# Gathers between two expert layers: from tile-by-tile waits to two in flight on two semaphores

## The chip, the core and the metric

The kernel runs on one core of a Trainium2 chip. The metric is the device time of one execution in microseconds (us); the time before is the median of three executions.

## The reference, cut to what matters

2048 tokens of 128 channels go through four residual layers: an attention, a mixture of 64 experts with 6 chosen per token, a table lookup, and a mixture of 8 experts with 2 chosen per token.

```python
x = x + attention(layernorm(x))
x = x + moe64(layernorm(x))      # sum over a token's 6 experts of weight * expert(token), + a shared expert
x = x + lookup(layernorm(x))     # offsets and weights from x, entries taken from x[0], summed, @ W_out + b_out
x = x + moe8(layernorm(x))       # sum over a token's 2 experts of weight * expert(token)
```

The change lies between the two expert layers: where each token's 6 expert outputs are brought together, and where the lookup and the router of the second mixture run on them.

## The kernel before

Tokens lie in 16 tiles of 128, in 4 chunks (q = 0 to 3) of 4 tiles. The engines have a program each, written out by hand, and wait for each other through named semaphores. An indirect DMA of the GpSimd engine (POOL) moves 128 rows, one per partition, by a column of row numbers, and adds 16 to a semaphore when it has landed.

1. During the attention, POOL scatters normalized tokens to slots in DRAM (`chunk_scatter`, line 1317, 96 scatters). Those of the chunks 0 to 2 wait on `exp_done`, three at a time; the last ones wait for nothing between them.
2. The 64 experts' layer runs over 80 pairs of slot blocks and writes its outputs to `y0_dram`.
3. Between the layers, `gathers(q, first, last)` (line 1374) brings the six outputs of each token into `GB`: 6 gathers for each tile, 24 for each chunk, 96 in all, 64 KB each. VectorE (DVE) waits for a tile's six in `combined(q, i)`, multiplies by the weights (line 1774), sums (1775), adds to `X` (1776) and takes statistics (1777). `moments_of` (1782) closes a chunk, POOL computes `rstd` from it (`chunk_scale`, 1382 and 1384), DVE normalizes (`scaled`, 1789), TensorE (PE) turns the rows (829), ScalarE (ACT) copies them out (1169), PE computes the lookup's offsets (839), DVE turns them into indices (`lookup_index`, 1799 to 1824), PE turns these (883), ACT casts them (1187), PE and DVE fill the lookup (`filled`, 905 and 1838 on), and `looked_up` adds the result. One chunk later the same tiles go through the second router (`router1_...`, lines 1870 to 1904; 1904 writes the slots).
4. `chunk_dispatch` (line 1392, 32 scatters) sends the tokens to the slots of the second mixture, whose 39 tiles end the kernel; each adds its rows to DRAM with one scatter (line 1418), which waits for the landing of the one two back, on `summed0` and `summed1` by turns.

What POOL does in the stretch between the layers is one queue in this order: 30 gathers (chunk 0 and the first tile of chunk 1), `chunk_scale` for chunk 0, 24 gathers, two `chunk_scale`, 24 gathers, two `chunk_scale`, 18 gathers, 4 dispatch scatters, two `chunk_scale`, the other scatters. DVE does, for q = 0 to 2: `scaled`, `combined(q + 1, 0)`, `lookup_index(q)`, `combined(q + 1, 1)`, `filled(q)`, `combined(q + 1, 2)`, `looked_up(q)`, `combined(q + 1, 3)`, with the router of the chunk before between them.

Of the kernel before, what the change touches and what calls it, by code (L numbers as in the profile page):

```python
# [12 lines left out]
P = 128  # L13
T = 2048
# [112 lines left out]
def build(nc, a, out):  # L127
# [12 lines left out]
    with ctx:  # L140
# [177 lines left out]

        TERMS_AT = (1, 2, 4, 5)
        SHIFT_AT = {1: 3, 3: 6}  # L320

        TURN_OF_LOOKUP = (0, 2, 4, 5)
# [167 lines left out]
        def _(pe):  # L490
# [67 lines left out]
            pe.wait_ge(sem("hxy_ready"), 1)  # L558
# [4 lines left out]
            last.then_inc(sem("corners_psum"), 1)  # L563
# [3 lines left out]
            pe.wait_ge(sem("corners_ready"), 1)  # L567
# [18 lines left out]
            pe.wait_ge(sem("mr_ready"), 1)  # L586
# [104 lines left out]
            pe.wait_ge(sem("q_final"), 1)  # L691
# [67 lines left out]
            mm(totals, cb("onesb"), earlier[:, :], start=False, stop=True, skip_group_check=True).then_inc(sem("totals0"), 1)  # L759
# [4 lines left out]
            pe.wait_ge(sem("table_cols"), 1)  # L764
# [87 lines left out]
            def counts1(q):  # L852
# [13 lines left out]
                if q == NC - 1:  # L866
                    for t in range(NT):
                        last = mm(totals1, cb("onesb"), MB[:, t, :], start=(t == 0), stop=(t == NT - 1), skip_group_check=True)
                    last.then_inc(sem("totals1"), 1)

            def tables():

                pe.wait_ge(sem("dx_ready"), 1)
                mm(PS[:, 7 * BANK:7 * BANK + P], cf("ones"), wout[:, :], start=True, stop=True)
                mm(PS[:, 7 * BANK + P:7 * BANK + P + 8], cf("selx"), dx[:, :], start=True, stop=True).then_inc(sem("tables_psum"), 1)
# [12 lines left out]
            def fills(q):  # L888
# [3 lines left out]
                for kind, i in FILLS:  # L892
# [16 lines left out]
                    else:  # L909
                        pe.wait_ge(sem("tables_ready"), 1)  # L910
# [321 lines left out]
        def _(pool):  # L1232
# [191 lines left out]
        def _(dve):  # L1424
# [80 lines left out]
            for c in range(NC):  # L1505
# [6 lines left out]
               hm[:, :].unsqueeze(2).to_broadcast([P, G, 2 * P]), ALU.mult).then_inc(sem("hxy_ready"), 1)  # L1512
            v.tensor_copy(XN[:, :, P:P + 1].bitcast(i32), cf("tok", 0, NT).unsqueeze(2)).then_inc(sem("rows_ready"), 1)
            dve.wait_ge(sem("corners_psum"), 1)
# [3 lines left out]
            STT(VV[:, :], vtb[:, :], cf("ksel")[:, 1:2], vtx[:, :], ALU.mult, ALU.add).then_inc(sem("corners_ready"), 1)  # L1518
# [14 lines left out]
            TT(low3, rest, middle, ALU.subtract).then_inc(sem("mr_ready"), 1)  # L1533
            dve.wait_ge(sem("mrows_psum"), 1)
            TT(QM[0][:, 0:T // 2], bank(0, 2), QS[0][:, 0:T // 2], ALU.add).then_inc(sem("q_final"), 1)
# [130 lines left out]
            def tiles_counted():  # L1666
# [3 lines left out]
                dve.wait_ge(sem("totals0"), 1)  # L1670
# [7 lines left out]
            def table_columns():  # L1678
# [10 lines left out]
                TS_(tcol[:, 1, :], tcol[:, 1, :], float(BLOCKS0), None, ALU.min).then_inc(sem("table_cols"), 1)  # L1689
# [365 lines left out]
```

## Time and profile before

| | |
|---|---|
| median of three executions | 970.17 us (969.85 to 970.34) |
| profiled execution, first to last instruction | 955.8 us |
| DVE busy in it | 640.0 us (67%) |
| POOL busy in it | 439.0 us (46%), of which 93.6 us are the 96 gathers |

The span leaves out what lies before the first and after the last instruction; the median of the runs is 14.4 us above it. The profiled execution's own time beyond its span is not shown.

How to read it: in a row of the timeline, the first number is the start in us, the second how long the instruction (or the merged run of instructions, with their count) took; in brackets is the time that the engine stood idle before it, and what ended it. "issue" is idle time for which the profile shows no other releaser, "remote" a releaser that it can't name.

### The profile page before, as it was taken

What the parts mean: (1) busy time and instruction counts of PE and PEld (TensorE: products, weight loads), DVE (VectorE), ACT (ScalarE), POOL (GpSimd) and SP (SyncE); (2) the same over time, 40 slices, a digit from 0 to 9 for tenths busy, and PEclk for the clock granted to TensorE, in tenths of its full rate; (3) what the DMA queues carried; (4) which work ended last, traced back from release to release, by engine and by line L of the source; (5) the groups of instructions that cost most, each with busy time, mean ns of one, the idle gap of its engine ahead of it and who ended that gap; (6) DMA issues with size and microseconds to landing.
All of it is one profiled execution on the core that took longest, in us unless ns stands there. A gap on an engine that the chain in (4) does not pass through costs nothing.

```text
span 955.8 us, 17380 instructions
## 1 busy us (share of the span) xinstructions
PE 691.5 (72%) x5945; PEld 406.9 (43%) x5945; DVE 640.0 (67%) x1333; ACT 451.2 (47%) x620; POOL 439.0 (46%) x674
## 2 busy tenths in 40 slices
PE   4799999999989988657999992024243462599992
PEld 3322223222222223225889992011212132599992
DVE  6899998999989878625767642345757774144442
ACT  4788888778877877301444441000001010356550
POOL 4220011542352245472767775772647354255552
PEclk9999999999999999977999997555555555699997
DMA  8999999999993000522987662210111011133336
GB/s 253 292 300 309 309 309 309 303 292 290 309 360 156 1 29 26 134 79 53 277 256 193 169 172 62 53 47 19 47 31 47 26 49 38 39 49 50 48 47 146
DMA packets 83479, 142.91 MB, mean 150 GB/s; under 512 B 10736, under 2 KB 75728, under 8 KB 81888
## 3 DMA queue, kind: packets, MB, share of 16 engines
q1 hardware_dynamic: 57744, 118.07, 41.4%
q0 software_dynamic: 12784, 17.40, 8.0%
q10 hardware_dynamic: 12864, 6.33, 2.4%
q8 instruction: 49, 0.80, 0.4%
q14 instruction: 38, 0.31, 0.1%
HBM read 116.57 MB, written 101.34 MB: 228 GB/s over the span
## 4 chain that ended last, share of the span: by engine, by line
PE 52%; DVE 14%; issue 11%; ACT 8%; DMA 6%; another core or an unknown queue 3%; POOL 3%; SPq 2%; POOLq 0%; DVEq 0%; ACTq 0%
PE PS L637 12%; PE PS L622 8%; PE PS L969 7%; PE PS L611 6%; ACT PB L1103 4%; DMA XP<-slots_scratch 3%; PE PS L979 3%; PE PS L805 3%; PE PS L792 2%; PE PS L794 2%; DVE routed L1775 2%; POOL slots_scratch L1392 2%; PE PS L780 1%; DVE GB L1774 1%
## 5 line engine op out<-in xcount | busy, mean ns | idle before, releaser
L1614 DVE TENSOR_SCALAR PS<-PS 128x1024 f32<-128x1024 f32 x244 | 290.8, 1228 | 30.7 <-PE PS L611 26.0
L1103 ACT ACTIVATE PB<-PS 128x1024 f32<-128x1024 f32 x224 | 226.8, 1026 | 55.5 <-PE PS L622 46.9
L637 PE MATMUL PS<-PB,VS 128*32 128x256 f32 x2048 | 163.8, 392 | 0.2 <-ACT PB L1106 0.2
L1317 POOL DMA_INDIRECT slots_scratch<-XN,slot x96 | 92.9, 967 | 64.7 <-ACT PB L1103 35.4
L611 PE MATMUL PS<-QS,KP 64*128 64x512 bf16 (+1 forms) x576 | 99.3, 360 | 24.6 <-ACT PB L1103 14.5
L1374 POOL DMA_INDIRECT GB<-y_scratch,slotc x96 | 93.6, 975 | 36.3 <-issue 28.6
L622 PE MATMUL PS<-QM,KP 64*128 64x512 bf16 (+1 forms) x576 | 100.3, 363 | 2.7 <-DVE PS L1614 2.6
L1418 POOL DMA_INDIRECT sums_scratch<-YO,XG x39 | 60.7, 1557 | 61.7 <-DVE YO L1982 60.5
L969 PE MATMUL PS<-XTT,WB 128*128 128x128 f32 x624 | 78.4, 281 | 0.0
L969 PEld LDWEIGHTS PS<-XTT,WB 128*128 128x128 f32 x624 | 75.1, 197 | 0.5 <-issue 0.5
L622 PEld LDWEIGHTS PS<-QM,KP 64*128 64x128 bf16 x576 | 25.1, 93 | 104.7 <-DVE PS L1614 59.5
L637 PEld LDWEIGHTS PS<-PB,VS 128*32 128x32 f32 x2048 | 40.4, 108 | 66.3 <-issue 65.4
L1358 POOL COPY WQ<-W0GU 128x192 f32 x160 | 55.4, 346 | 25.3 <-issue 22.9
L829 PE MATMUL PS<-CF,XN 128*128 128x128 f32 x32 | 8.9, 434 | 75.4 <-DVE XN L1789 75.4
L1325 POOL TENSOR_TENSOR X<-X,TQ 128x256 f32<-128x256 f32 x7 | 5.1, 726 | 118.5 <-DVE TQ L1544 118.5
L1169 ACT COPY XT<-PS 128x512 f32<-128x512 f32 x8 | 4.7, 586 | 114.4 <-PE PS L829 114.4
L1975 DVE COPY XTT<-PS 128x128 f32<-128x128 f32 x39 | 11.4, 292 | 70.6 <-PE PS L957 70.6
L611 PEld LDWEIGHTS PS<-QS,KP 64*128 64x128 bf16 x576 | 25.9, 93 | 72.6 <-ACT PB L1103 52.7
L1216 ACT COPY WB<-W1GU 128x1024 f32 x39 | 40.7, 1046 | 22.7 <-PE PS L969 14.9
L1158 ACT ACTIVATE SP<-PS 96x256 f32<-96x256 f32 x80 | 30.4, 380 | 42.6 <-PE PS L794 42.6
L1135 ACT COPY YP<-PS 128x256 f32<-128x256 f32 x80 | 29.8, 373 | 35.2 <-PE PS L805 35.1
L1226 ACT ACTIVATE SG<-PS 128x512 f32<-128x512 f32 x39 | 23.3, 597 | 43.1 <-PE PS L969 27.9
(289 smaller groups left out, 1322.6 us busy)
## 6 DMA issues: line engine op xcount, KB each, us to landing
y_scratch<-YP SPq DMA_DIRECT2D x80, 128.0 KB, 2.5
slots_scratch<-slots_scratch SPq DMA_DIRECT2D x1, 8768.0 KB
W0GU<-in_w0gu SPq DMA_DIRECT2D x1, 6144.0 KB
XP<-slots_scratch SPq DMA_DIRECT2D x80, 64.0 KB, 2.7
XP<-slots_scratch ACTq DMA_DIRECT2D x80, 64.0 KB, 2.7
W1GU<-in_w1gu SPq DMA_DIRECT2D x8, 512.0 KB, 4.0
W0D<-in_w0d SPq DMA_DIRECT2D x1, 3072.0 KB
XG<-slots_scratch SPq DMA_DIRECT2D x39, 68.5 KB
```

Source lines behind the costliest of these rows:

```text
L611: last = mm(o, keys, QS[g][r, x], start=first, stop=True, skip_group_check=not first)
L622: last = mm(o, keys, QM[g][r, x], start=False, stop=True, skip_group_check=True)
L637: last = mm(PS[32 * j:32 * j + 32, at:at + HALF], VS[:, n, g * HG + j, :], PB[u // 2 % 3][:, 2 * (j % 2) + j // 2, q], start=(n == 0 and h ...
L969: last = mm(PS[:, at + k * P:at + (k + 1) * P], WB[j % 2][:, w], XTT[j % 2][:, :], start=True, stop=True)
L1103: A(PB[u // 2 % 3][:, 2 * hp:2 * hp + 2, :], pair_banks(u).rearrange("p (j q) -> p j q", j=2), ACT.Exp).then_inc(sem("exp_done"), 1)
L1158: A(SP2[i % 2][:, 0:2 * P], PS[0:H0, (2 + i % 2) * BANK:(2 + i % 2) * BANK + 2 * P], ACT.Silu).then_inc(sem("pair_silu"), 1)
L1216: nc.scalar.copy(WB[j % 2][:, :], W1GU[:, ds(expert, 1), :].squeeze(1)).then_inc(sem("w_placed"), 1)
L1317: gp.indirect_dma_start(slots0_dram.rearrange("b p d -> (b p) d"), bass.IndirectOffsetOnAxis(ap=slot0[:, t, k:k + 1], axis=0), XN[:, t, 0: ...
L1358: gp.tensor_copy(WQ[j % 6][:, :], W0GU[:, ds(expert, 1), :].squeeze(1)).then_inc(sem("wq_ready"), 1)
L1374: gp.indirect_dma_start(GB[:, t, k, :], None, y0_dram.rearrange("b p d -> (b p) d"), bass.IndirectOffsetOnAxis(ap=slotc[:, t, k:k + 1], ax ...
L1418: gp.indirect_dma_start(sums_dram[j % 2][:, :], bass.IndirectOffsetOnAxis(ap=XG[j % NXG][:, P:P + 1].bitcast(i32), axis=0), YO[j % 4][:, : ...
L1614: TS_(pair_banks(u), pair_banks(u), 4.0, 0.0, ALU.mult, ALU.max).then_inc(sem("relu_done"), 1)
```

## The change

Each gather, counted through as g = 6 t + k, now adds to `gathered0` or `gathered1` by turns, and before it is issued POOL waits for the landing of gather g - 2. Before, POOL waited only at the first gather of a tile, for the landing of the tile four back, and the semaphores went by tiles (four of them). DVE waits for a tile's six gathers with two waits, one on each semaphore, in place of one. Besides, eleven semaphores that were each used once are replaced by two that count up (`single_ready`, raised seven times by DVE, and `single_psum`, raised four times by PE); each waiter waits for the value that its producer's instruction raises it to. The scatters of the second dispatch (line 1392) stay as they are in this diff.

```diff
+        CORNERS_PSUM, TOTALS0, TABLES_PSUM, TOTALS1 = 1, 2, 3, 4
+        HXY_READY, CORNERS_READY, MR_READY, Q_FINAL, TABLE_COLS, DX_READY, TABLES_READY = 1, 2, 3, 4, 5, 6, 7
+        IN_FLIGHT = 2
...
-            pe.wait_ge(sem("hxy_ready"), 1)
+            pe.wait_ge(sem("single_ready"), HXY_READY)
...
-            last.then_inc(sem("corners_psum"), 1)
+            last.then_inc(sem("single_psum"), 1)
...
                     t, k = 4 * q + n // TOP0, n % TOP0
-                    if t >= 4 and k == 0:
-                        pool.wait_ge(sem(f"gathered{t % 4}"), 16 * TOP0 * (t // 4))
+                    g = TOP0 * t + k
+                    if g >= IN_FLIGHT:
+                        pool.wait_ge(sem(f"gathered{g % IN_FLIGHT}"), 16 * (g // IN_FLIGHT))
                     gp.indirect_dma_start(GB[:, t, k, :], None, y0_dram.rearrange("b p d -> (b p) d"),
                                           bass.IndirectOffsetOnAxis(ap=slotc[:, t, k:k + 1], axis=0)).then_inc(
-                                              sem(f"gathered{t % 4}"), 16)
+                                              sem(f"gathered{g % IN_FLIGHT}"), 16)
...
                 t = 4 * q + i
-                dve.wait_ge(sem(f"gathered{t % 4}"), 16 * TOP0 * (t // 4 + 1))
+                for g in range(IN_FLIGHT):
+                    dve.wait_ge(sem(f"gathered{g}"), 16 * (TOP0 // IN_FLIGHT) * (t + 1))
                 rows = GB[:, t, :, :]
```

The other lines of the diff replace the remaining single-use semaphores in the same way.

## Rows read from the trace of the kernel before

**Rows 1.** The page: the span, and the chain that ended last, by engine.
```profile
span 955.8 us, 17380 instructions
...
PE 52%; DVE 14%; issue 11%; ACT 8%; DMA 6%; another core or an unknown queue 3%; POOL 3%; SPq 2%; POOLq 0%; DVEq 0%; ACTq 0%
```

**Rows 2.** The timeline of POOL from 583 to 718 us.
```profile
583.05 1.01 POOL L1374 DMA_INDIRECT GB<-y_scratch,slotc  x1 [7.68 <-DMA y_scratch<-YP]
...
620.35 0.26 POOL L1382 TENSOR_SCALAR rstd<-moments 128x4 f32<-128x4 f32 x1
...
621.94 1.08 POOL L1374 DMA_INDIRECT GB<-y_scratch,slotc  x1 [0.20 <-issue]
...
651.93 0.94 POOL L1374 DMA_INDIRECT GB<-y_scratch,slotc  x1 [0.30 <-issue]
670.38 0.84 POOL L1382 TENSOR_SCALAR rstd<-moments 128x4 f32<-128x4 f32 x1 [17.51 <-DVE moments L1782]
...
717.96 0.84 POOL L1382 TENSOR_SCALAR rstd<-moments 128x4 f32<-128x4 f32 x1 [12.17 <-DVE moments L1782]
```

**Rows 3.** Line 1374 by itself: durations min/median/max in ns, first and last start.
```profile
L1374 POOL DMA_INDIRECT GB<-y_scratch,slotc x96: 941/945/1589, 583.1 to 744.3; - x96
```

**Rows 4.** Timelines of DVE, PE and ACT, from 617 to 676 us.
```profile
617.62 0.38 DVE L1782 BATCH_NORM_AGGREGATE moments<-stats 128x2 f32<-128x6 f32 x4
...
621.85 1.19 DVE L1789 TENSOR_SCALAR XN<-X,moments,rstd 128x128 f32<-128x128 f32 x4 [3.77 <-issue]
...
655.46 0.75 DVE L1838 TENSOR_SCALAR OH<-PS,CF 128x512 f32<-128x512 f32 x1 [5.20 <-PE PS L905]
...
675.15 1.25 DVE L1789 TENSOR_SCALAR XN<-X,moments,rstd 128x128 f32<-128x128 f32 x4 [0.47 <-POOL rstd L1384]
...
624.89 1.97 PE L839 MATMUL PS<-wol,XT 128*128 128x64 f32 x8 [0.68 <-ACT XT L1169]
...
643.57 1.09 PE L883 MATMUL PS<-CF,TS 128*96 128x128 f32 x4 [15.95 <-issue]
...
652.65 0.58 ACT L1187 CAST TI<-PS 64x512 bf16<-64x512 f32 x1 [20.75 <-remote]
```

**Rows 5.** Busy time (and count) of PE, PEld, DVE, ACT, POOL in one stretch.
```profile
626.90:655.40 28.50, 3.92 (x13) 2.03 (x12) 8.04 (x25) 1.47 (x3) 19.87 (x21) 0.50 0.19 49
```

**Rows 6.** DVE's waits from 583 to 823 us: total us, times, longest.
```profile
DVE routed L1775 <- remote: 5.2, 3, 1.8
DVE slot L1904 <- remote: 4.5, 1, 4.5
```

**Rows 7.** Timelines of PE, POOL and DVE at the last scatters of `chunk_scatter`.
```profile
413.06 2.05 PE L747 MATMUL PS<-wshd,HP 96*128 96x128 f32 x16 [0.84 <-DVE HP L1656]
...
428.02 0.96 POOL L1317 DMA_INDIRECT slots_scratch<-XN,slot  x1 [0.30 <-issue]
...
429.65 0.69 DVE L1661 TENSOR_TENSOR X<-X,PS 128x512 f32<-128x512 f32 x1 [14.88 <-remote]
```

**Rows 8.** Timelines of POOL and ACT among the scatters paced by `exp_done`.
```profile
358.29 0.96 POOL L1317 DMA_INDIRECT slots_scratch<-XN,slot  x1 [1.27 <-ACT PB L1106]
...
363.11 0.96 POOL L1317 DMA_INDIRECT slots_scratch<-XN,slot  x1 [1.23 <-ACT PB L1106]
...
364.40 1.02 ACT L1106 ACTIVATE PB<-PS 128x1024 f32<-128x1024 f32 x1 [0.65 <-PE PS L622]
```

**Rows 9.** The chain that ended last, in order of time: start, length.
```profile
589.38 2.47 DMA GB<-y_scratch,slotc
...
915.26 3.30 DMA sums_scratch<-YO,XG
...
939.43 3.40 DMA sums_scratch<-YO,XG
```

**Rows 10.** The timeline of POOL at the last scatters of line 1418.
```profile
935.45 1.55 POOL L1418 DMA_INDIRECT sums_scratch<-YO,XG  x1 [0.30 <-issue]
...
939.43 1.55 POOL L1418 DMA_INDIRECT sums_scratch<-YO,XG  x1 [0.31 <-issue]
```

More of the change, by code:

```diff
@@ L585, in _ @@
                 mm(bank(c), cb("identb"), QS[0][:, c * CH:(c + 1) * CH], start=True, stop=False, skip_group_check=True)
-            pe.wait_ge(sem("mr_ready"), 1)
+            pe.wait_ge(sem("single_ready"), MR_READY)
             for g in range(G):
@@ L689, in counts0 @@
                 last.then_inc(sem("counts0_psum"), 1)
-            pe.wait_ge(sem("q_final"), 1)
+            pe.wait_ge(sem("single_ready"), Q_FINAL)
             scores(0)
@@ L758, in _ @@
                 mm(totals, cb("onesb"), chosen[:, NT - 2 + t, :], start=(t == 0), stop=False, skip_group_check=True)
-            mm(totals, cb("onesb"), earlier[:, :], start=False, stop=True, skip_group_check=True).then_inc(sem("totals0"), 1)
+            mm(totals, cb("onesb"), earlier[:, :], start=False, stop=True, skip_group_check=True).then_inc(sem("single_psum"), 1)
             shared_down(0)
@@ L763, in _ @@
             shared(2)
-            pe.wait_ge(sem("table_cols"), 1)
+            pe.wait_ge(sem("single_ready"), TABLE_COLS)
             for k in range(2):
@@ L868, in counts1 @@
                         last = mm(totals1, cb("onesb"), MB[:, t, :], start=(t == 0), stop=(t == NT - 1), skip_group_check=True)
-                    last.then_inc(sem("totals1"), 1)
+                    last.then_inc(sem("single_psum"), 1)
             def tables():
-                pe.wait_ge(sem("dx_ready"), 1)
+                pe.wait_ge(sem("single_ready"), DX_READY)
                 mm(PS[:, 7 * BANK:7 * BANK + P], cf("ones"), wout[:, :], start=True, stop=True)
-                mm(PS[:, 7 * BANK + P:7 * BANK + P + 8], cf("selx"), dx[:, :], start=True, stop=True).then_inc(sem("tables_psum"), 1)
+                mm(PS[:, 7 * BANK + P:7 * BANK + P + 8], cf("selx"), dx[:, :], start=True, stop=True).then_inc(sem("single_psum"), 1)
             def weights_turned(q):
@@ L909, in fills @@
                     else:
-                        pe.wait_ge(sem("tables_ready"), 1)
+                        pe.wait_ge(sem("single_ready"), TABLES_READY)
                         pe.wait_ge(sem("filled_dve"), 9 * q + 2 + 2 * i)
@@ L1517, in _ @@
             step(v.tensor_copy(vtb[:, :], vtx[:, :]))
-            STT(VV[:, :], vtb[:, :], cf("ksel")[:, 1:2], vtx[:, :], ALU.mult, ALU.add).then_inc(sem("corners_ready"), 1)
+            STT(VV[:, :], vtb[:, :], cf("ksel")[:, 1:2], vtx[:, :], ALU.mult, ALU.add).then_inc(sem("single_ready"), 1)
             bound, above, rest = (small[:, i, :] for i in range(3))
@@ L1532, in _ @@
             step(v.tensor_copy(middle, rest))
-            TT(low3, rest, middle, ALU.subtract).then_inc(sem("mr_ready"), 1)
+            TT(low3, rest, middle, ALU.subtract).then_inc(sem("single_ready"), 1)
             dve.wait_ge(sem("mrows_psum"), 1)
-            TT(QM[0][:, 0:T // 2], bank(0, 2), QS[0][:, 0:T // 2], ALU.add).then_inc(sem("q_final"), 1)
+            TT(QM[0][:, 0:T // 2], bank(0, 2), QS[0][:, 0:T // 2], ALU.add).then_inc(sem("single_ready"), 1)
             def sums_scaled(p, b):
@@ L1949, in _ @@
             router1_slots(NC - 1)
-            dve.wait_ge(sem("totals1"), 1)
+            dve.wait_ge(sem("single_psum"), TOTALS1)
             step(TT(passed[:, :, :], PS[:, 5 * BANK:5 * BANK + E1].unsqueeze(2).to_broadcast([P, E1, NT]),
```

16 lines of the change are left out of this document (8 added, 8 removed).

## The prediction, made before the changed kernel was run

> **What bounds the kernel now.** I read the page first: the chain that ended last runs through PE for half the span, but 3% of it goes to "another core or an unknown queue", on a kernel that has one core [rows 1]. That line was the first thing to explain. Then POOL's timeline between the two expert layers, where the changed instructions are [rows 2]; the same stretch on DVE, PE and ACT [rows 4]; and, since the trace of before has no gather that waits for the one two back, the rows of scatters that do [rows 10] and the landings in the chain [rows 9].
>
> POOL's queue sets the end of the first part of this stretch. The 96 gathers take 0.945 us each [rows 3], with 0.30 us between them [rows 2], so one starts every 1.25 us. DVE has closed chunk 0 at 617.62 + 0.38 = 618.00 us [rows 4], but `chunk_scale` stands behind 30 gathers and starts at 620.35 [rows 2]; DVE's normalization follows at 621.85 [rows 4]. In the next two chunks POOL is done early: it idles 17.5 and 12.2 us until DVE's moments come [rows 2].
>
> What makes DVE late there is not its work. PE's offsets end at 624.89 + 1.97 = 626.9 us, and from there to 655.4 us DVE is busy for 8.0 of 28.5 us [rows 4, 5]. ACT's cast waits for four transposes that ended at 643.57 + 1.09 = 644.7 and starts at 652.65, 8.0 us late, just as POOL issues its last gather of the series (651.93 + 0.94 = 652.9) [rows 2, 4]. The same picture stands at the last scatters of the first dispatch: PE's work ended at 415.1, the DVE instruction that waits for it starts at 429.65, 0.7 us after the last of a series of back-to-back scatters (428.02 + 0.96) [rows 7]. So I read it thus: while POOL issues indirect DMAs back to back, semaphore updates of the other engines can be held, and they come out when POOL stops. In the chunks 1 and 2 the holds are single ones on DVE, one of 4.5 us before line 1904 in each (the second, as long, stands under "issue") and one of 5.2/3 = 1.7 us before line 1775 [rows 6].
>
> **Term 1, the wait itself (a cost).** A gather's landing comes 2.47 us after its start [rows 9]. How soon POOL starts the next after a landing is read from line 1418, which already has this form: its last scatters start 939.43 - 935.45 = 3.98 us apart, two back [rows 10], and two of them land after 3.30 and 3.40 us [rows 9]; the difference is 0.68 or 0.58, so I take 0.63. Two gathers then take 2.47 + 0.63 = 3.10 us in place of 2.50. Bounds: 2.77 if POOL restarts after the usual 0.30 us; 3.38 if the scatter's whole 3.98 holds, less only the difference of the instructions (1.55 - 0.95). I take 3.10, the reading nearest in form.
>
> The Trainium skill (DMA: Bandwidth & Descriptors, section on the anatomy of a SWDGE DMA) gives about 2.0 us plus bytes at 436 GB/s for a DMA issued from GpSimd. For 64 KB that is an estimate of 2.15 us; the trace has 2.47. By the page the cycle would be 2.78 and the first chunk's cost 14 x 0.28 = 3.9 us.
>
> **Term 2, the first chunk.** The thirty gathers ahead of the first `chunk_scale` hold 14 waits in a row on either semaphore: 14 x 0.60 = +8.4 us, all on the path, since DVE's last tile of the chunk (11 cycles, +6.6) is ready at 624.6 and `chunk_scale` comes at 628.8. Queued behind the waiting gathers on POOL are only `chunk_scale` and the dispatch; who waits for them is DVE's normalization.
>
> **Term 3, the holds (a gain).** With 3.10 us per two gathers POOL stands still for 3.10 - 1.25 - 0.95 = 0.9 us in each cycle. Is this enough to let the updates out? The nearest rows are the paced scatters: three in 363.11 - 358.29 = 4.8 us, with a pause of 1.23 us [rows 8]. There ACT waits 0.65 us for PE, and no wait of several us stands in that series of 17 scatters; the hold after the last unpaced scatter ended 0.7 us after POOL did [rows 7]. So I take it that 0.9 us is enough, that holds fall from many us to under 1 us, and keep the other answer as a rival. In the first chunk the stretch of 28.5 us shrinks to DVE's 8.0 us of work and some 0.9 us of true waits: -19.6 us [rows 5].
>
> **Term 4, where the gain stops.** DVE would then bring the moments of the next scale at 670.3 + 8.4 - 19.6 = 659.1 us. But POOL's series of 24 gathers starts at 621.94 + 8.4 = 630.3 and takes 1.35 + 11 x 3.10 + 0.95 = 36.4 us, until 666.7. The slack of 17.5 us is used up and POOL is the bound again. The scale starts 3.7 us earlier than at 670.38, the second one right behind it, so that DVE's second normalization comes at 666.7 + 2.75 = 669.5 in place of 675.15: -5.7 us in all so far. In chunk 1 the same happens: the series ends at 669.6 + 36.4 = 706.0, DVE's moments (with its 6.3 us of holds gone) would come at about 706; the scale starts at 706.1 in place of 717.96, and with the second one right behind (2.75 us where there were 4.8) the shift is -13.9 us. In chunk 2 only 18 gathers and 4 scatters stand in the series, they end before DVE's moments (which have 12 us of slack today), and the 6.3 us of holds come off in full: -20.2. The dispatch scatters after it are as before.
>
> **Edits at no cost.** DVE's second wait per tile is one more semaphore instruction, 16 in all; both are raised by gathers that landed before, except in the first chunk, where the last landing decides as now. Below nothing it can't be; above, 16 times the 0.03 to 0.2 us between dependent DVE instructions, under 3 us if nothing covered it; I take 0. The merged semaphores are raised by the same instructions in the same order on one engine each, so every wait ends when it did; neither a gain nor a loss has a way in. No DMA or SP instruction is added or moved; SP's queue waits for `x_lookup` and `dispatched`, which come earlier or later with the chain.
>
> **Sum.** 955.8 + 8.4 - 14.1 (of the 19.6, what POOL's series leaves) - 8.2 - 6.3 = 935.6 us, that is -20.2. I add 1.5 us for short holds that stay: -18.7, a span of 937. The runs' median stands 14.4 us above the span [rows 1], which I carry over: 970.2 - 18.7 = 951.5, **forecast 951 us**. Its own range is 944 to 960: with the cycle at 2.77 the same steps give -26.5, with 3.38 they give -10.
>
> **Rivals.**
> - Holds stay (slower). They come from the rate of indirect DMAs over a long series, not from the missing pause: before, the first one in a series came some 5 us in (PE's update at 626.9, after 30 gathers nearly without a break). Then term 3 falls away; the cost is 8.4 us if the holds keep their lengths, and as they end with the series, whose 24 gathers take 5.5 us more, up to 14: **979 to 984 us**. For it speaks that 1.55 us per gather is still less than the 1.6 us of the densest paced series; against it, that in that series POOL's pauses do end the waits. It decides wherever the pause is too short for an update to pass.
> - Only the holds that reach to the series' end go (ACT's cast, PE's updates); DVE's single ones of 4.5 and 1.7 us stay, in both later chunks. Chunk 1 loses 6.3 of its gain and chunk 2 all of its own: -5.7 at the first, nothing more: **about 964 us**.
> - The change doesn't do what it says: POOL looks ahead, the landing two back is there when it asks, and the cycle is 2.77 with a pause of 0.57 us, below the 0.7 us that the release took [rows 7]. Cost 14 x 0.27 = 3.8, holds as now: **974 us**.
> - The holds exist only in the profiled execution. Then the timed runs have only the cost: +8.4 in the first chunk, and 5.5 in the second, where without holds POOL's series was the bound before too: **984 us**. Against it: 14.4 us between span and timed runs leave no room for some 30 us of holds that only the profile has. The Trainium skill (NOTIFIC — the notification-queue block, section on overflow) says that a full path of trace records can stall its producers, which is the way in which this could be; no run here shows it yet.
>
> **How the numbers follow.** Forecast 0.53; partial release 0.13; holds stay 0.20; no effect of the wait 0.03; only in the profile 0.06; the rest, 0.05, is a cancelling of cost and partial gain near today's time. Faster by over 0.2% is 0.53 + 0.13 = 0.66, slower 0.20 + 0.03 + 0.06 = 0.29, within 0.2% 0.05; 0.2% (2 us) is about what a measurement of this kernel can tell. Cases of both signs hold most of the chance, so the range goes from the forecast's lower end to the slow rivals: 943 to 984.
>
> **What the profile after would show.** Gathers two back start 3.1 us apart, with idle time ended by the DMA. The first scale starts near 628.8 us. Line 1799 follows PE's offsets at once, ACT's cast stands behind line 883 by 0.1 us, lines 1904 and 1775 have no "remote" wait of over 1 us. `chunk_scale` after the second and third series starts right after the last gather. The hold at 415 to 429 us stays as it is. I am wrong if DVE's idle time between 627 and 655 us remains, or if a landing's wait costs POOL much more than 0.63 us.

## The result and the profile after

The changed kernel takes **936.92 us** (median of 4 executions, 935.43 to 939.77). The kernel before, run beside it on the same chip, takes 970.25 us (969.85 to 974.32). The ratio is 0.966, with a 95% interval of 0.962 to 0.969. The forecast of 951 us was 14 us too high, and the time lies 6 us below the range of 943 to 984: the direction was right, the size wrong. Here and below, a few executions far above their kernel's others (1092, 2186 and 3436 us) are left out.

**The page** of the changed kernel, for [rows 1]:

```profile
span 935.6 us, 17392 instructions
...
PE 54%; DVE 12%; DMA 11%; ACT 8%; issue 6%; POOL 4%; another core or an unknown queue 2%; SPq 2%; POOLq 0%; DVEq 0%; ACTq 0%
```

This execution's own time was 937.44 us, so only 1.8 us lie outside its span. The share of "another core or an unknown queue" went from 3% to 2%, that of DMA from 6% to 11%, that of "issue" from 11% to 6%: the gathers' landings are now a link of the chain.

**POOL's timeline** between the expert layers, for [rows 2] (line 1378 holds the gathers, 1386 the scale):

```profile
590.93 1.01 POOL L1378 DMA_INDIRECT GB<-y_scratch,slotc  x1 [7.61 <-DMA y_scratch<-YP]
592.24 0.95 POOL L1378 DMA_INDIRECT GB<-y_scratch,slotc  x1 [0.30 <-issue]
593.65 0.95 POOL L1378 DMA_INDIRECT GB<-y_scratch,slotc  x1 [0.46 <-DMA GB<-y_scratch,slotc]
595.05 0.95 POOL L1378 DMA_INDIRECT GB<-y_scratch,slotc  x1 [0.45 <-DMA GB<-y_scratch,slotc]
...
600.50 1.64 POOL L1378 DMA_INDIRECT GB<-y_scratch,slotc  x1 [0.45 <-DMA GB<-y_scratch,slotc]
...
635.63 0.26 POOL L1386 TENSOR_SCALAR rstd<-moments 128x4 f32<-128x4 f32 x1
...
671.02 0.25 POOL L1386 TENSOR_SCALAR rstd<-moments 128x4 f32<-128x4 f32 x1
...
710.27 0.23 POOL L1386 TENSOR_SCALAR rstd<-moments 128x4 f32<-128x4 f32 x1 [1.36 <-DVE moments L1787]
```

Two gathers back, the distance is 595.05 - 592.24 = 2.81 us, with some 0.45 us of idle time before each of the two, ended by the DMA. Now and then a gather itself is longer (1.64 us at 600.50). Before the scale at 671.02 POOL no longer idles for DVE; it did for 17.51 us. The landings of the gathers in **the chain that ended last** (start, length), for [rows 9]:

```profile
592.24 2.55 DMA GB<-y_scratch,slotc
595.05 2.40 DMA GB<-y_scratch,slotc
597.72 2.53 DMA GB<-y_scratch,slotc
600.50 3.10 DMA GB<-y_scratch,slotc
```

The gather of 592.24 lands at 594.79, and POOL starts the one two on at 595.05, 0.26 us later. **DVE, PE and ACT** in the first chunk, for [rows 4], and the busy times (with counts) of PE, PEld, DVE, ACT and POOL in the stretch that answers to [rows 5]:

```profile
637.13 1.19 DVE L1794 TENSOR_SCALAR XN<-X,moments,rstd 128x128 f32<-128x128 f32 x4 [5.17 <-POOL rstd L1388]
...
642.17 0.42 DVE L1804 TENSOR_TENSOR OL<-PS,bol 128x256 f32<-128x256 f32 x1 [0.65 <-PE PS L842]
...
650.74 1.40 DVE L1843 TENSOR_SCALAR OH<-PS,CF 128x512 f32<-128x512 f32 x2
...
647.36 1.09 PE L886 MATMUL PS<-CF,TS 128*96 128x128 f32 x4 [4.46 <-issue]
...
648.48 0.58 ACT L1190 CAST TI<-PS 64x512 bf16<-64x512 f32 x1 [4.70 <-PE PS L886]
```

```profile
642.10:650.70 8.60, 3.47 (x13) 2.12 (x13) 7.98 (x25) 1.47 (x3) 6.13 (x7) 0.50 0.17 48
```

DVE does the same 25 pieces of work, 8.0 us, in 8.6 us in place of 28.5. TensorE's granted clock is 0.50 of full speed in both stretches (the first number behind POOL's), that is 1.2 GHz, so the clock is not what changed. ACT's cast starts 0.03 us after PE's four transposes end; it had come 8.0 us late. What is left of **waits** for a "remote" releaser in the whole kernel (total, times, longest), for [rows 6] and [rows 7]:

```profile
ACT SP L1131 <- remote: 20.4, 1, 20.4
DVE X L1665 <- remote: 17.6, 1, 17.6
...
DVE PS L1618 <- remote: 5.9, 4, 1.7
```

No line of the stretch between the layers is among them. The two long ones are those of [rows 7], at the unpaced scatters that the change doesn't touch, and the short ones lie in the attention.

A measure that takes out what lies ahead of the change is the time from the first gather to the end of the span: before 955.8 - 583.05 = **372.8 us**, after 935.6 - 590.93 = **344.7 us**, so -28.1. The first gather starts anywhere from 583 to 595 us in profiles whose code is the same up to there. I call this measure the stretch, and use it below beside the medians.

### The profile page after: what moved, and what is told of

It reads as the page before. It is cut to its first block, busy times and chain, and to the rows that moved or that the text cites. A ratio compares the mean times of both kernels' runs of the same rounds, so it can differ in the third digit from the quotient of the medians.

```text
span 935.6 us, 17392 instructions
## 1 busy us (share of the span) xinstructions
PE 690.7 (74%) x5944; PEld 405.9 (43%) x5945; DVE 640.6 (68%) x1333; ACT 451.1 (48%) x620; POOL 440.8 (47%) x674
## 4 chain that ended last, share of the span: by engine, by line
PE 54%; DVE 12%; DMA 11%; ACT 8%; issue 6%; POOL 4%; another core or an unknown queue 2%; SPq 2%; POOLq 0%; DVEq 0%; ACTq 0%
PE PS L640 12%; PE PS L625 9%; PE PS L972 8%; PE PS L614 7%; DMA GB<-y_scratch,slotc 6%; ACT PB L1106 4%; PE PS L982 3%; DMA XP<-slots_scratch 3%; PE PS L808 3%; PE PS L795 2%; PE PS L797 2%; POOL slots_scratch L1396 2%; PE PS L783 1%; DVE routed L1780 1%
## 5 line engine op out<-in xcount | busy, mean ns | idle before, releaser
L1618 DVE TENSOR_SCALAR PS<-PS 128x1024 f32<-128x1024 f32 x244 | 291.2, 1228 | 37.2 <-PE PS L614 28.5
L640 PE MATMUL PS<-PB,VS 128*32 128x256 f32 x2048 | 165.8, 396 | 0.2 <-ACT PB L1109 0.2
L614 PE MATMUL PS<-QS,KP 64*128 64x512 bf16 (+1 forms) x576 | 99.5, 361 | 28.4 <-ACT PB L1106 18.4
L1378 POOL DMA_INDIRECT GB<-y_scratch,slotc x96 | 96.0, 1000 | 49.7 <-DMA GB<-y_scratch,slotc 30.5
L614 PEld LDWEIGHTS PS<-QS,KP 64*128 64x128 bf16 x576 | 26.3, 94 | 75.7 <-ACT PB L1106 54.3
L832 PEld LDWEIGHTS PS<-CF,XN 128*128 128x128 f32 x32 | 5.7, 217 | 90.2 <-DVE XN L1794 90.2
```

The lines of the kernel that those rows point to most:

```text
L614: last = mm(o, keys, QS[g][r, x], start=first, stop=True, skip_group_check=not first)
L640: last = mm(PS[32 * j:32 * j + 32, at:at + HALF], VS[:, n, g * HG + j, :], PB[u // 2 % 3][:, 2 * (j % 2) + j // 2, q], start=(n == 0 and h ...
L1618: TS_(pair_banks(u), pair_banks(u), 4.0, 0.0, ALU.mult, ALU.max).then_inc(sem("relu_done"), 1)
```

## The experiments

Every kernel was timed beside the kernel before on its chip. Its median there went from 963 to 975 us from call to call, so medians are compared within a call, and across calls only ratios and stretches.

**1. The kernel before, once more.** No edit.

> The kernel before, unchanged, for a second trace of it. Holds theory: the timed runs of before are 12 us or more longer than the one traced execution (970.2 against a span of 955.8), because the holds of semaphore updates are not equally long in each execution; a second trace then shows a span some 1.8 us below its own time and longer holds, near 968 us in all. Rival (what lies around the span was 14.4 us and is now 1.8, a matter of the measurement): the second trace is again near 956 us with a time near 970.

It took 959.88 us, with a span of 958.0: again 1.9 us outside, and its stretch is 373.3. The holds are there (20.8 us on ACT's cast, 16.3 us on line 1661). So the 14.4 us that I had carried over from span to median were not something around the span. They were the difference between two executions. The other half of the expectation failed: the holds between the layers were no longer than in the first trace (373.3 us for 372.8), and the time was 959.88 us, not near 968.

**2. The merged semaphores alone.** The change without its edits to the gathers.

> Only the eleven single-use semaphores are merged into two; the gathers and their waits are those of before. Holds theory: the same instructions raise and await in the same order, so it takes the time of before, ratio 1.000 within 0.003. Rival (the merged semaphores give part of the gain, for instance because fewer semaphores or other numbers of them change when updates pass): a ratio clearly below 1, down to 0.987 if it is the part that the forecast missed.

962.32 us, ratio 0.999 (0.995 to 1.002), stretch 370.6, all holds there. The merge shows no cost and no gain.

**3. The gathers alone.** The kernel before with only these edits, and with the increments and DVE's waits that belong to them:

```diff
-                    if t >= 4 and k == 0:
-                        pool.wait_ge(sem(f"gathered{t % 4}"), 16 * TOP0 * (t // 4))
+                    if g >= IN_FLIGHT:
+                        pool.wait_ge(sem(f"gathered{g % IN_FLIGHT}"), 16 * (g // IN_FLIGHT))
```

> Only the gathers change (two in flight on two semaphores); the single-use semaphores stay. Holds theory: all of the gain, near 937 us. Rival (merging helps): between 940 and 955 us.

935.98 us, ratio 0.968 (0.963 to 0.973), stretch 346.5. This is the whole effect.

**4. Three in flight.** One number of the change:

```diff
-        IN_FLIGHT = 2
+        IN_FLIGHT = 3
```

> The changed kernel with three in flight: POOL asks for the landing of the gather three back, which is there already (2.5 us against 3.75), so gathers start every 1.25 us as before, with 0.30 us between them, but each still has a wait and the semaphores go by turns. Pause theory (only a longer stop of POOL lets the other engines' updates out): the holds are back, near 970 us. Rival (the wait by itself, or short counts on the semaphores, is what helps): no holds and a first chunk 4 us shorter, near 933 us.

958.49 us, ratio 0.994 (0.990 to 0.998), stretch 371.1. POOL's timeline, and two of the waits:

```profile
600.71 0.94 POOL L1378 DMA_INDIRECT GB<-y_scratch,slotc  x1 [0.30 <-issue]
```

```profile
ACT TI L1190 <- remote: 16.6, 1, 16.6
ACT WE L1196 <- remote: 10.0, 1, 10.0
```

The landing three back is there when POOL asks, the pause is 0.30 us again, and the holds are back. The wait for a landing by itself does little if anything: the ratio allows 0.2 to 1.0%, and the stretch, taken from the slowest of the ten executions (966.04 us), shows 1.7 us.

**5. The pause without the landing.** The gathers as before; behind each a memset of 10 columns of a tile that is dead by then, for which the next gather waits:

```diff
+                    if g >= 1:
+                        pool.wait_ge(sem("rested"), g)
...
+                    gp.memset(<10 columns of keyed>, 0.0).then_inc(sem("rested"), 1)
```

> Gathers wait for landings as before (tile four back), but behind each gather POOL clears ten columns of a tile that is not used any more and the next gather waits for that: a stop of about 0.45 us between gathers in place of 0.30, and no wait for a landing. Pause theory: the stop is what counts, the holds are gone or nearly so, 935 to 942 us. Rival (no more than two gathers under way is what counts; at one gather per 1.4 us the landing two back is there anyway, so this would count as two in flight too, but nothing enforces it): holds come back where a landing is late, 945 to 965 us.

940.03 us, ratio 0.968 (0.964 to 0.972), stretch 345.2. POOL's timeline:

```profile
601.13 1.71 POOL L1380 DMA_INDIRECT GB<-y_scratch,slotc  x1 [0.27 <-POOL keyed L1383]
...
604.18 0.12 POOL L1383 MEMSET keyed<- 128x10 f32 x1
604.57 0.95 POOL L1380 DMA_INDIRECT GB<-y_scratch,slotc  x1 [0.27 <-POOL keyed L1383]
```

Between two gathers lie 0.12 + 0.27 = 0.39 us, in place of 0.30. There is no "remote" wait between the layers. About a tenth of a microsecond more between indirect DMAs does what the change does. It doesn't come alone, though: three of the first thirty gathers take 1.63 to 1.71 us, as at 601.13, and one pause lasts 1.63 us, so that most gathers start 1.35 us apart but the mean is 1.49. The runs don't separate the small pause from these.

**6. One in flight** (IN_FLIGHT = 1).

> The changed kernel with one gather in flight: each waits for the landing of the one before, a cycle of 2.75 us per gather in place of 1.38. Both theories: no holds between the layers; the cost is POOL's queue: thirty gathers ahead of the first scale take 41 us more than with two in flight, the next 24 take 33 us more of which DVE's work hides nothing (it needs some 35 us, the series then lasts 66), so about 41 + 30 + 30 + 15 us more: 1030 to 1065 us. It shows what a landing costs POOL by itself.

1062.25 us, ratio 1.093 (1.090 to 1.097), stretch 467.6:

```profile
603.88 0.94 POOL L1378 DMA_INDIRECT GB<-y_scratch,slotc  x1 [1.75 <-DMA GB<-y_scratch,slotc]
```

The idle time of 1.75 us in each of 96 gathers, with POOL's series as the bound, is what a real wait for a landing costs; the holds stay away as with two.

**7. Two in flight in the unpaced scatters too** (the last 24 of the first dispatch, and five of chunk 2). All scatters count on two semaphores by turns.

```diff
+                    if pace is None and g >= 2:
+                        pool.wait_ge(sem(f"scattered0_{g % 2}"), 16 * (g // 2))
```

> The changed kernel, and the unpaced scatters of the first dispatch (29 of 96: five of chunk 2, and the last 24) also two in flight on two semaphores. Holds theory: DVE's 17 us and ACT's 20 us of waits at the end of the scatters (one after the other ends, both by the series' end) go; the series of 24 gets 24 x 0.13 = 3 us longer, and the experts can't start before its last landing. The last landing now comes some 7.5 us after the last scatter's start and PE, DVE and ACT still have about 11 us of the shared expert's work to do after it; with the holds gone that work is done before: 8 to 12 us less, 925 to 930 us. Rival (the experts' start hangs on the last scatter's landing alone): 3 us more, 940 us.

938.48 us, ratio 0.966 (0.962 to 0.971), neither of the two numbers. From the waits, and from the timeline of POOL:

```profile
DVE X L1670 <- remote: 11.8, 2, 9.3
```

```profile
419.41 0.96 POOL L1325 DMA_INDIRECT slots_scratch<-XN,slot  x1 [8.88 <-DMA slots_scratch<-XN,slot]
420.67 0.96 POOL L1325 DMA_INDIRECT slots_scratch<-XN,slot  x1 [0.30 <-issue]
```

Past one long wait, a scatter's landing two back is nearly always there and the pause stays at 0.30 us. DVE still waits 9.3 us at one place; ACT's one wait of 20 us has become several of 4.6 to 9.1 us. The time is that of the changed kernel. No trace shows the 7.5 us from the last scatter to its landing that the expectation names; where the chain has this landing (experiment 17, 433.32 us), it takes 2.23. Here waiting for a landing is the wrong means; it gives no pause.

**8. Two in flight in all scatters of the first dispatch.** The same wait without `pace is None`.

> As the run with the last scatters, and the paced scatters of the chunks 0 to 2 also wait for the landing two back, beside their pace of three per four or three pairs. Holds theory: PE's short holds of 0.6 to 1.7 us in the attention, which the traces show at each third scatter, get shorter or go: a further 3 to 8 us less. Rival (the pause after each three already lets them out, and what is left is not on the path): the time of the run with the last scatters, within 2 us.

1000.74 us, ratio 1.030 (1.027 to 1.033): a miss. POOL's timeline, and busy times of PE, PEld, DVE, ACT and POOL by stretch, then the granted clock and the DMA share:

```profile
182.90 0.96 POOL L1325 DMA_INDIRECT slots_scratch<-XN,slot  x1 [11.17 <-DMA slots_scratch<-XN,slot]
...
204.28 0.96 POOL L1325 DMA_INDIRECT slots_scratch<-XN,slot  x1 [6.58 <-DMA slots_scratch<-XN,slot]
...
225.27 0.96 POOL L1325 DMA_INDIRECT slots_scratch<-XN,slot  x1 [5.56 <-DMA slots_scratch<-XN,slot]
```

```profile
170.00:230.00 60.00, 55.80 (x558) 16.53 (x556) 52.26 (x48) 48.39 (x49) 8.16 (x9) 0.99 0.99 301
230.00:290.00 60.00, 0.00 (x0) 0.00 (x0) 0.00 (x0) 0.00 (x0) 11.52 (x12) 0.50 0.97 334
```

There the DMA engines are 97 to 99% busy, nearly all of it with other transfers, and a scatter's landing is 7.0 to 13.1 us away in the chain. With the wait POOL issues 9 instructions in 60 us, falls behind, and PE, DVE and ACT stand still for the next 60 us. Behind it the kernel is the changed one: the stretch is 344.8 us. The same edit is harmless, useless or ruinous by what the landing waits for.

**9. The first 30 gathers free.** As experiment 5, with the memset only behind gathers 30 to 95.

> No gather waits for the one two back. The first 30 gathers stand as before (0.30 us between them), and behind each of the other 66 a 10-column memset gives the 0.40 us of pause. Theory that the short pause between gathers is all that counts, and that the first 30 need none (no engine's update was needed in the first 5 us of holds there): the first normalization comes back by 3 to 7 us against the changed kernel, the holds between 627 and 655 us stay away, and the time is 930 to 934. Rival: a hold begins while the first 30 run back to back and lasts on, or the holds return in the next series: 945 to 960.

949.86 us beside 974.55, ratio 0.976 (0.971 to 0.981), stretch 351.9. The theory that the short pause between two gathers is all that counts fell. The first scale came 630.74 - 593.47 = 37.3 us after the first gather, as hoped, but then, on PE, DVE, ACT and POOL:

```profile
635.27 1.97 PE L842 MATMUL PS<-wol,XT 128*128 128x64 f32 x8 [0.67 <-issue]
...
641.70 0.43 DVE L1808 TENSOR_TENSOR OL<-PS,bol 128x256 f32<-128x256 f32 x1 [5.07 <-remote]
...
649.45 0.29 DVE L1831 TENSOR_TENSOR TS<-TS,lmax 128x128 f32<-128x128 f32 x1 [1.67 <-remote]
...
652.98 1.09 PE L886 MATMUL PS<-CF,TS 128*96 128x128 f32 x4 [14.98 <-DVE TS L1833]
...
657.24 0.58 ACT L1190 CAST TI<-PS 64x512 bf16<-64x512 f32 x1 [13.93 <-remote]
...
661.19 1.06 PE L902 MATMUL PS<-TW,CF 32*128 32x512 f32 x1
...
667.21 0.58 ACT L1196 COPY WE<-PS 128x512 f32<-128x512 f32 x1 [2.96 <-remote]
...
678.33 0.84 POOL L1391 TENSOR_SCALAR rstd<-moments 128x4 f32<-128x4 f32 x1 [10.77 <-DVE moments L1791]
```

These holds lie in a series whose gathers all have the pause. PE's offsets end at 635.27 + 1.97 = 637.24 and reach DVE 4.5 us late; the cast came 3.2 us after its transposes (652.98 + 1.09 = 654.07); and some twenty paused gathers in, the matmul that ends at 662.25 reaches ACT 5.0 us late. The same series after paused gathers has none of this (experiment 5), so they are left over from the unpaused thirty, and the pauses of the series don't visibly work them off. In the next series, after POOL has idled for 10.8 us, they are gone.

**10. A pause behind every third gather.**

> The memset stands behind every third gather only; two gaps of 0.30 us and one of 0.40 us, mean distance 1.28 us. Theory of a dose (updates come out in any gap that is long enough): the holds last at most three gathers, 4 us, few of them matter, and the time is 936 to 942. Rival (the load must drain over the whole series, so the mean rate counts): the holds stay in part, remote waits of ACT and DVE of 5 to 20 us, and the time is 950 to 962, as with three gathers in flight.

949.85 us, ratio 0.975 (0.970 to 0.980), stretch 353.6: the lower end of the rival's range. Holds stay: 10.6 us in two waits of DVE on line 1851, and others of 1 to 3 us. The first thirty gathers take 39.4 us, one per 1.31 us; unpaused they take 37.3 (1.24), with the change 44.7 (1.49). The holds on line 1851 stand in the next 24, which start 1.37 us apart on average; with the change these start 1.43 us apart.

**11. The second dispatch, two in flight,** which the change leaves as it was. Its scatters count on two semaphores by turns.

```diff
+                        if g >= 2:
+                            pool.wait_ge(sem(f"dispatched{g % 2}"), 16 * (g // 2))
```

> The changed kernel, with the 32 scatters of the second dispatch two in flight as well, which the diff leaves as they were. Theory: their landings come before POOL asks (scatters to DRAM land sooner than gathers), only 4 of them stand between engines that wait, and the time is that of the changed kernel, 935 to 940. Rival: the wait makes the last scatters later and the second expert layer with them, 32 times up to 0.3 us: 940 to 948.

943.92 us beside 974.55, ratio 0.968 (0.963 to 0.973), which is that of the changed kernel. The time lies in the rival's range of 940 to 948, but this chip's kernel before was slow too. The stretch is 349.0, some 2 to 4 us longer. It gains nothing; a cost of up to 4 us can't be excluded.

**12. Experiment 9 with the pause in the unpaced scatters as well:** a memset of 5 columns behind each of the last 24, for which the next one waits.

```diff
+                    if s >= 3:
+                        gp.memset(<5 columns of pairsum>, 0.0).then_inc(sem("tail_rested"), 1)
```

> As the kernel with the first 30 gathers free, and a 5-column memset also behind each of the 24 unpaced scatters at the end of the first dispatch. Theory that a pause of 0.40 us between indirect DMAs ends the holds wherever they are: the remote wait of 15 to 18 us on line 1665's form in that place and that of ACT of 20 us go down to under 3 us, the scatters take 3 us more, and the time is 3 to 12 us under that of the kernel with the first 30 free, 920 to 930. Rival (there the holds hide behind the transfers that the expert layer's beginning waits for): same time within 3 us. Rival (a pause of 0.40 us is too short for scatters): the holds stay and the time is 3 us longer.

938.11 us, ratio 0.966 (0.961 to 0.971), against 0.976 without it in the same call: 11.8 us less. The waits of 17.3 and 20.4 us are gone; those of 5.1 and 13.1 us in the first chunk are as in experiment 9 (5.1 and 13.9). The range of 920 to 930 us was missed; the gain lies in the forecast 3 to 12 us, but the kernel of experiment 9 stood at 950, not at 930 to 934.

**13. The changed kernel with that pause.**

> The changed kernel, and a 5-column memset behind each of the 24 unpaced scatters at the end of the first dispatch. If the two places add, what the pause gave there on the kernel with the first 30 free (0.9763 to 0.9661 of the kernel before, some 10 us) comes off here too: ratio 0.955 to 0.960, 925 to 931 us. Rival (they share one gain): ratio 0.963 to 0.969, 935 to 942 us.

927.73 us beside 963.13, ratio 0.965 (0.961 to 0.968). The time is in the first range, the ratio in the rival's, because this chip's kernel before was faster. It decides nothing; experiments 16 and 17 do.

**14. One long rest.** Experiment 9 with eight memsets of 300 columns between the first scale and gather 30:

```diff
+                if q == 1:
+                    for i in range(8):
+                        if i >= 1:
+                            pool.wait_ge(sem("long_rest"), i)
+                        gp.memset(<300 columns of keyed>, 0.0).then_inc(sem("long_rest"), 1)
```

> The kernel with the first 30 gathers free and a memset behind each of the other 66, and eight memsets of 300 columns in a row (2.5 to 4 us) between the first normalization's scale and gather 30. Theory of a backlog that piles up in unpaused gathers and drains in pauses: the rest empties it, DVE gets PE's offsets without the 5.1 us, the casts of ACT come without the 3 us, and the time is 8 to 14 us under that of the kernel without the long rest: ratio 0.962 to 0.968. Rival (no backlog; in this stretch 0.40 us is too short a pause for another reason): the holds stay and the time is that of the kernel without it, ratio 0.974 to 0.980.

932.26 us beside 963.13, ratio 0.970 (0.965 to 0.975), between the two ranges of the expectation, and its interval reaches into both; stretch 339.9. POOL, DVE and ACT:

```profile
627.63 3.31 POOL L1415 MEMSET keyed<- 128x300 f32 x8
...
632.85 0.42 DVE L1813 TENSOR_TENSOR OL<-PS,bol 128x256 f32<-128x256 f32 x1 [0.67 <-PE PS L842]
...
639.37 0.58 ACT L1190 CAST TI<-PS 64x512 bf16<-64x512 f32 x1 [4.91 <-issue]
```

After 3.3 us of rest, PE's update reaches DVE at once, and no hold is left between the layers. The ratio doesn't decide it; these rows do. The stretch is 12.0 us shorter than that of experiment 9 and 4.8 us shorter than that of the changed kernel.

**15. The first 30 gathers paused, all others back to back.**

> The memset stands behind the first 30 gathers alone, all later ones are back to back at 0.30 us. Theory of a backlog: the second series starts with an empty one, its first waits are short, and holds grow with the number of gathers since: under 1 us at DVE's wait for PE's offsets (6 gathers in), many us at ACT's cast. Time 950 to 962, ratio 0.975 to 0.992. Rival (each gap decides for itself, with no memory): the holds are those of before from the first one on, and the 4.5 us of pauses come on top: ratio 1.00 to 1.01.

947.93 us beside 963.13, ratio 0.985 (0.980 to 0.990), stretch 357.9: the ratio as expected, the time 2 us below its range. DVE's and POOL's timelines:

```profile
633.48 0.42 DVE L1808 TENSOR_TENSOR OL<-PS,bol 128x256 f32<-128x256 f32 x1 [0.65 <-PE PS L842]
...
654.83 1.16 DVE L1868 SCALAR_TENSOR_TENSOR X<-cw,PS,X 128x128 f32<-128x128 f32 x4 [0.94 <-remote]
...
682.83 0.23 DVE L1913 TENSOR_SCALAR slot<-top 128x8 int32<-128x8 f32 x1 [3.58 <-remote]
...
705.73 0.84 POOL L1391 TENSOR_SCALAR rstd<-moments 128x4 f32<-128x4 f32 x1 [12.32 <-DVE moments L1791]
...
731.77 0.17 DVE L1913 TENSOR_SCALAR slot<-top 128x8 int32<-128x8 f32 x1 [4.53 <-remote]
```

The first series behind starts with nothing piled up, and its holds stay under 1 us through 24 unpaused gathers; ACT's cast, for which I had expected many us, had none. In the two series after it they are 3.6 and 4.5 us. The theory said that holds grow with the number of gathers since the last pause, and that is not borne out: 24 gathers in a row did next to nothing, and then the last series, which starts at 710.64 after POOL has idled for 12.3 us, has a hold of 4.5 us after only 13. The kernel before shows the same in its third series: POOL had idled for 17.5 us [rows 2], the series starts at 675.30, and DVE's wait of 4.5 us before line 1904 begins at 691.91, after 13 gathers. Something besides the count matters, perhaps what else runs: these two series carry the router's instructions too, the one with next to nothing doesn't. No run separates this. (One gather of the thirty, and three of the next 24, were long ones here, which thins the series out.)

**16, 17, 18. Three versions on one chip,** beside a kernel before of 964.00 us: the changed kernel, the same with the pause in the unpaced scatters, and experiment 14 with that pause.

> The changed kernel, unedited, as the measure for the other two on the same chip. Ratio 0.963 to 0.970.

> The changed kernel with the pause in the unpaced scatters, beside the changed kernel on the same chip. If the places add, it is 6 to 10 us under it. If the expert layer waits for the landing of the last scatters, which come 3 us later with the pauses, it is 0 to 4 us under it.

> Gathers 0 to 29 back to back, the long rest of 3.3 us, memsets behind the other 66, and the pause in the unpaced scatters. Backlog theory: the first part of the stretch ends at the earliest (first scale 37 us after the first gather in place of 45), no hold is left in the kernel outside the attention, and it is 3 to 8 us under the kernel of the run before this one. Rival: in the first chunks POOL's series of gathers is the bound anyway, and the two are the same within 2 us.

| | median us | ratio (95%) | first gather | stretch |
|---|---|---|---|---|
| 16, the change | 938.07 | 0.975 (0.972 to 0.977) | 587.63 | 345.7 |
| 17, with the scatters' pause | 930.20 | 0.965 (0.963 to 0.968) | 579.54 | 346.1 |
| 18, long rest and scatters' pause | 924.27 | 0.959 (0.957 to 0.962) | 579.34 | 339.9 |

The ratio of 16 misses its expectation of 0.963 to 0.970 and lies clear of the first measurement's interval (0.962 to 0.969): the gain of the change is 2.5 to 3.4%, by the chip and the call. The places add: in the profiles 8.1 us come off ahead of the gathers (17 against 16) and 6.2 us from the first gather on (18 against 17); by the medians it is 7.9 and 5.9 us, both as expected. The first copy of the expert layer starts at 446.88 us in 16. In 17 POOL's timeline has it right behind the last pause, and the waits for a "remote" releaser are only these:

```profile
434.29 0.12 POOL L1329 MEMSET pairsum<- 128x5 bf16 x1
434.33 0.35 POOL L1369 COPY WQ<-W0GU 128x192 f32 x1
```

```profile
DVE PS L1626 <- remote: 1.7, 1, 1.7
ACT PB L1109 <- remote: 0.7, 1, 0.7
```

Of the 12.6 us by which the layer starts earlier it gives 4.5 us back. **Version 18 is the fastest of all, 39.7 us under the kernel before and 13.8 us under the changed one.**

## Why the prediction was right and wrong

**What bounds the kernel: right.** DVE was late because other engines' finished work reached it late while POOL issued indirect DMAs close together. Experiments 4 and 5 show that the distance between these decides, with and without a wait for a landing. That it is the semaphore updates that are held is my reading of the rows; what holds them no run shows.

**Term 1, the cycle: mis-sized.** I took 3.10 us for two gathers. Where neither is a long one they take 2.67 to 2.81 (595.05 to 597.72, 592.24 to 595.05): POOL restarts 0.25 to 0.27 us after a landing, not 0.63. The larger value came from line 1418, whose instruction is longer; I chose "the reading nearest in form" where the lower bound of 2.77 held. Averaged over a series, with the long gathers, two take 3.02 us in the first and 2.85 in the second and third. The Trainium skill (DMA: Bandwidth & Descriptors, section on the anatomy of a SWDGE DMA) gave 2.78; the rows without a long gather agree for the cycle, but its 2.15 us for the landing does not (2.40 to 2.55), so the match comes from the restart.

**Term 2, the first chunk: nearly right, by luck.** The scale came 44.7 us after the first gather in place of 37.3, so +7.4 (predicted +8.4). POOL's thirty gathers were busy for 31.2 of the 44.7 us, and for 28.4 of the 37.3 before. So 2.8 us are longer gathers (four of these thirty took about 1.64 us), which the sum didn't have, and 13.5 - 8.9 = 4.6 us are pauses. Of these, 1.6 are one pause of 1.92 us before the gather of 617.00, for which the profile names no cause; the other 3.0 are what the waits cost. Experiment 5, without the wait, had three such gathers and such a pause; the unpaused thirty of before and of experiment 14 had none.

**Term 3, the holds: right in the first chunk, too small in the later ones.** From the first normalization to line 1843 DVE needs 13.6 us in place of 33.6: -20.0, predicted -19.6. But POOL's idle time is not one pause of 0.9 us in each cycle, as I had argued; it falls before every gather, some 0.45 us each, and 0.39 us does it as well (experiment 5). So the rival that a pause of 0.57 us is too short lost: what counts is not the length of one pause against that of a release. In the two later chunks I counted 6.3 us of holds each. From one second normalization to the next DVE needs 47.6 us before and 37.9 after, then 44.2 and 36.0: -9.7 and -8.1, for which the sum had -8.2 and -6.3. I had overlooked a hold in the trace of before, and called the holds there "single ones":

```profile
696.45 0.17 DVE L1904 TENSOR_SCALAR slot<-top 128x8 int32<-128x8 f32 x1 [4.54 <-remote]
...
709.07 0.75 DVE L1842 SCALAR_TENSOR_TENSOR AW<-PS,CF,WE 128x512 f32<-128x512 f32 x1 [3.34 <-remote]
```

After the change the second of these waits is 1.65 us, for PE's work. Besides, in each chunk four waits of 0.3 to 0.7 us of DVE behind its own earlier instructions, 1.9 us together, were gone; I had put them at nothing.

**Term 4, POOL as the next bound: right for the second series, a tie in the third.** POOL goes from the last gather of each series straight to the first scale, as forecast, but in the third it then waits 1.36 us for DVE's moments before the scale at 710.27. From the first gather on, the shift is -9.3 us at DVE's second normalization (predicted -5.7), -19.0 at the scale of 710.27 (predicted -13.9), and -27.1 at the next (predicted -20.2). With the cycle at 2.77 "the same steps give -26.5"; measured were -28.1, and -26.3 and -27.1 in experiments 3 and 16. That the two ends meet is partly luck: by those steps, as I redo them, the second normalization would shift by 13.9 us, and it shifted by 9.3; the larger holds of the later chunks make up for it.

**Edits at no cost: right** (experiment 2).

**The hold at [rows 7]: stayed,** as forecast (17.6 and 20.4 us), and was worth another 8 us (experiment 17).

**Sum: where the 14 us come from.** Forecast was -18.7, the two medians differ by 33.3. In the stretch the change gave 28.1, that is 9.4 more: 3.6 up to DVE's second normalization (1.0 in the first chunk, and 2.6 by the shorter cycle in the series behind it), 1.5 and 1.8 by the holds of the two later chunks, which term 3 had too small, 1.5 that I had left for short holds, of which none stayed, and 1.0 behind these chunks that I can't assign. The other 5.2 us lie outside the stretch or between executions: the same comparison of medians gave 29.2 us in experiment 3 and 25.9 us in experiment 16. My range had no room for this spread. The step "the runs' median stands 14.4 us above the span, which I carry over" was false as well: an execution's time is its span plus 1.8 us, and the traced one (about 957.6 us) was a low one of a kernel whose executions lay between 956 and 981 us over all calls. It did not move the forecast, which is a difference from the median, but it hid that spread from me, and an argument rested on it (next).

**The rivals.** Holds stay: false. Only the long ones go: false. POOL looks ahead: the distance that it gave, 2.77, was about right, its conclusion wrong. Holds only in the profiled execution: **my argument against it was void.** It rested on the 14.4 us. Moreover every execution timed here comes with a span and a granted clock, that is, it was recorded too; no run shows the kernel without recording. What the runs do show is that something piles up over thirty indirect DMAs 1.25 us apart, still delays updates some twenty paused gathers later, and is gone after one rest of 3.3 us (experiments 9 and 14); and that the number of gathers is not all that it depends on (experiment 15). Records of the trace would be a candidate for such a pile. The Trainium skill (NOTIFIC — the notification-queue block, section on overflow) says that the block's inner path holds its producers back rather than lose a record; no run here separates this from a pile of the DMAs' own work, and it stays open.

## What to carry to other kernels

When an engine waits for a "remote" releaser while another engine had long finished, look at what POOL was doing: a long series of indirect DMAs without a pause is the suspect. Try a tiny independent instruction (0.1 us) behind each, for which the next one waits, or one rest of 3 us where POOL has slack. The rest clears what has piled up; it doesn't protect an unpaused series behind it (4.5 us of wait after 13 gathers, experiment 15). A wait for a landing works only where the landing happens to come late enough, costs 1.75 us per DMA where it comes later, and stops the whole kernel where the DMA engines are full. Compare the part of the span that begins at the change, and do not carry a difference between one traced execution and a median over into a forecast.

## What the runs showed of the hardware that was not expected

- The delay of other engines' updates has a memory: after 30 gathers 1.25 us apart, an update in the next series, whose gathers had their pauses, came 4.5 us late, and another one still 5.0 us late some twenty gathers on; a rest of 3.31 us between the two series removed the delays (experiments 9 and 14).
- A small change of the mean distance decides. At one gather per 1.25 us waits of up to 20 us stand on ACT; in experiment 10, at 1.31 us in the first series and 1.37 in the second, some of 5 us stay; at 1.42 us and more, from the first gather on, none is left (the change, experiment 5). These means hold gathers of 1.6 to 1.7 us; most gathers of experiment 5 start 1.35 us apart.
- Some gathers take 1.64 to 1.7 us in place of 0.945: four of the first thirty with the change, three with the memset, none when they run back to back. Their landings take 3.10 us in place of 2.5. I don't know why.
- An indirect scatter lands in 2.23 us in one place (the last unpaced one of experiment 17) and in 7.0 to 13.1 us where the DMA engines are 97 to 99% busy (experiment 8).
